# A reordered output phase: row maxima, moments, convolution and merge take other places in their engines' queues

## The reference, cut to what matters

```python
b, n, d = x.shape                       # 16 images, 4096 tokens, 128 channels
h, m, dh = (8, 64, 16)                  # heads, landmarks, width of a head
sim1 = jnp.einsum('bhid,bhjd->bhij', q, k_l)
attn1 = jax.nn.softmax(sim1, axis=-1)
out = attn1 @ attn2_inv @ (attn3 @ v)   # the last two factors: 64 x 16 a head, made earlier
res = conv_general_dilated(v, conv_w, ...)   # 33 taps along the tokens, a filter a head
out = out + res
out = out.transpose(0, 2, 1, 3).reshape(b, n, h * dh)
return x + (out @ w_out + b_out)
```

## Time and profile before

| | us |
|---|---|
| median of 3 runs | 5909.45 |
| the profiled execution, its own time | 5913.64 |
| its span | 5911.8 |
| output phase, first to last reciprocals of full slots | 2542.9 to 3561.8 |
| TensorE busy in the whole span | 5253.6 |
| ScalarE busy in the whole span | 3138.0 |
| VectorE busy in the whole span | 3071.2 |

### The profile page before, as it was taken

The page is one execution under the profiler, slowest core; times in us unless marked ns, Lnnn a source line. Parts: engine busy times, 40 slices in busy tenths (PEclk is TensorE's granted clock), DMA queues, the critical chain, the costliest instruction groups (busy, mean ns, idle before and its releaser), DMA issues. The chain is left out here.

```text
span 5911.8 us, 223297 instructions
## 1 busy us (share of the span) xinstructions
PE 5253.6 (89%) x97395; PEld 3278.2 (55%) x97488; DVE 3071.2 (52%) x8152; ACT 3138.0 (53%) x9108; POOL 1523.0 (26%) x1905
## 2 busy tenths in 40 slices
PE   5599999997899998799999997888888888888888
PEld 4599888896566666744444444333333333333333
DVE  8677777775788886568888883111111111111111
ACT  6465555565677776378888883333333333333333
POOL 2100000002888874256666662000000000000000
PEclk7899999999999999999999998999999999999999
DMA  9631111225777773467777762111111111111100
GB/s 389 270 115 58 58 58 60 84 77 183 245 245 243 231 243 105 102 175 203 202 203 202 204 173 66 33 34 32 32 34 33 32 32 35 32 32 32 35 18 24
DMA packets 773031, 689.32 MB, mean 117 GB/s; under 512 B 67056, under 2 KB 663024, under 8 KB 767984
## 3 DMA queue, kind: packets, MB, share of 16 engines
q1 hardware_dynamic: 754672, 575.39, 32.6%
q0 software_dynamic: 14672, 95.16, 4.0%
q10 hardware_dynamic: 2736, 4.89, 0.2%
HBM read 392.17 MB, written 274.89 MB: 113 GB/s over the span
## 5 line engine op out<-in xcount | busy, mean ns | idle before, releaser
L2797 ACT ACTIVATE f_y<-f_acc 128x16 f32<-128x16 f32 x4096 | 754.7, 184 | 1542.5 <-PE f_acc L2739 1542.5
L2739 PEld LDWEIGHTS f_acc<-f_y,f_vT 128*32 128x32 f32 x32768 | 645.2, 108 | 1438.7 <-ACT f_y L2797 1437.0
L2739 PE MATMUL f_acc<-f_y,f_vT 128*32 128x16 f32 x32768 | 1046.1, 193 | 279.6 <-issue 1.5
L2697 PE MATMUL f_junk<-f_idle 128*32 128x512 bf16 x8400 | 832.5, 376 | 0.0
L2579 DVE COPY f_zT<-f_zt 128x512 f32<-128x512 f32 x124 | 85.8, 692 | 1138.4 <-PE f_zt L2653 1138.4
L2355 DVE TENSOR_REDUCE o_m<-o_bank_l 128x8 bf16<-128x512 f32 x512 | 329.7, 686 | 132.4 <-PE o_bank_l L2152 130.0
L2572 DVE TENSOR_SCALAR f_wxn<-f_wxp,f_scale,f_shift 128x512 f32<-128x512 f32 x126 | 102.1, 811 | 509.0 <-PE f_wxp L2667 508.9
L1299 ACT ACTIVATE a_p<-a_s 128x512 f32<-128x512 f32 x502 | 259.3, 602 | 153.0 <-PE a_s L1166 151.2
L2318 ACT ACTIVATE o_p<-o_bank_s 128x512 f32<-128x512 f32 x512 | 264.4, 602 | 142.0 <-PE o_bank_s L2175 142.0
L533 POOL DMA_DIRECT2D hidden<-l_h x46 | 34.7, 756 | 1162.1 <-DVE l_hsum L790 961.6
L712 ACT ACTIVATE l_gate<-l_pf,r_ctx 128x256 f32<-128x256 f32 (+7 forms) x512 | 202.5, 446 | 229.1 <-PE l_pf L643 228.8
(11 more groups left out here) (323 smaller groups left out, 11517.6 us busy)
## 6 DMA issues: line engine op xcount, KB each, us to landing
o_v<-vals SPq DMA_DIRECT2D x256, 272.0 KB, 3.4
a_hid<-hidden SPq DMA_DIRECT2D x112, 520.0 KB, 5.0
hidden<-l_h POOLq DMA_DIRECT2D x46, 1040.0 KB, 6.6
l_x<-skew SPq DMA_DIRECT2D x46, 1024.0 KB, 5.2
vals<-a_v SPq DMA_DIRECT2D x128, 272.0 KB, 3.4
gn_x<-in_x SPq DMA_DIRECT2D x16, 2048.0 KB, 17.4
a_xin<-in_x SPq DMA_DIRECT2D x128, 256.0 KB, 5.1
tokens<-a_t SPq DMA_DIRECT2D x128, 256.0 KB, 3.4
```

The source lines that it names most:

```text
L2697: nc.tensor.matmul(junk[rows, :], idle[:, 0:QUAD], idle[:, :], start=True, stop=True)
L2739: mm = nc.tensor.matmul(acc[k % 2][rows, t, :], vT[:, rows], before, start=False, stop=True, skip_group_check=True)
L2797: nc.scalar.activation(y[q][:, step, :], acc[step // RC % 2][:, step % RC, :], ACT.Sigmoid).then_inc(s_y, 1)
```

## The change

Four things move; no instruction is added or taken away.

1. TensorE: the first half of `row_maxima` comes before `scores`; `moments` and `convolve` come before `weigh` instead of at the end; `turn_maxima` comes before `queries`. As the convolution now precedes `weigh`, it has a wait of its own for the first three exponentials, since it overwrites `bank_s[2]`.
2. ScalarE: `copy_convolved` comes before `copy_weighed`, `negate` before `copy_queries`.
3. VectorE: `merge` of chunk c-1 comes before `reciprocals` of chunk c-1 instead of at the end of the slot.
4. After the last slot `merge` and `reciprocals` swap in the same way.

```diff
@@ TensorE
             def slot(b, c, q, first, last):
-                scores(b, c, q)
                 nq = q if c + 1 < NG else 1 - q
                 if follows(c, 1, last):
                     row_maxima(b, c + 1, 0, nq)
+                scores(b, c, q)
                 if precedes(c, 3, first):
                     project(b, c - 3)
                 if follows(c, 1, last):
                     row_maxima(b, c + 1, 1, nq)
+                if precedes(c, 4, first):
+                    moments(b, c - 4)
+                if not last:
+                    wait(pe, "exp", PAIRS_H * nth(b, c) - 1)
+                    convolve(b + 1, c, bank_conv[:, :])
                 weigh(b, c, q)
+                if follows(c, 1, last):
+                    turn_maxima(b, c + 1)
                 if follows(c, 3, last):
                     queries(b, c + 3)
-                if follows(c, 1, last):
-                    turn_maxima(b, c + 1)
-                if not last:
-                    convolve(b + 1, c, bank_conv[:, :])
                 if precedes(c, 2, first):
                     turn_convolved(b, c - 2, q if c >= 2 else 1 - q)
-                if precedes(c, 4, first):
-                    moments(b, c - 4)
@@ ScalarE
+                if not last:
+                    copy_convolved(b + 1, c, 1 - q, bank_conv[:, :])
                 copy_weighed(b, c)
+                if follows(c, 1, last):
+                    negate(b, c + 1)
                 if follows(c, 3, last):
                     copy_queries(b, c + 3)
-                if follows(c, 1, last):
-                    negate(b, c + 1)
-                if not last:
-                    copy_convolved(b + 1, c, 1 - q, bank_conv[:, :])
@@ VectorE
                 if precedes(c, 1, first):
+                    merge(b, c - 1)
                     reciprocals(b, c - 1)
                 if precedes(c, 2, first):
                     normalise(b, c - 2)
                     add_convolved(b, c - 2)
-                if precedes(c, 1, first):
-                    merge(b, c - 1)
@@ VectorE, after the last slot
             residual(B - 1, NG - 3)
+            merge(B - 1, NG - 1)
             reciprocals(B - 1, NG - 1)
-            merge(B - 1, NG - 1)
```

## The result

The changed kernel takes 5947.33 us (median of 4 runs, 5929.85 to 5951.33), the kernel before 5909.9 (median of 4). The ratio is 1.0055, interval [1.0042, 1.0068]: slower, as forecast, 5 us under the 5952 given. The profiled execution of the changed kernel was its fastest run: 5929.85 us, span 5928.1.

A forecast was written before the change was run, and what follows sets the result against it. Bound: TensorE's 8.10 us a slot, 0.53 of it waits, and a chain through DRAM closing once a slot. -13 - 4 + 41 + 19 = +43 on 5913.64 gives 5957, less 4.2: 5952 us; 8-in-10 range 5892 to 5985.

The forecast's parts named there:

- The 0.53 us of waits: TensorE's waits for the row maxima's reduction and the last exponential go, 0.53 us a slot: pace 8.10 to 7.57.
- The copies behind weigh: Scores wait for the queries' copy, now fourth on ScalarE behind `weigh`: 0.06 us lost a slot, pace 7.63.
- The turn through DRAM: Reciprocals, spread, pack and next reciprocals close once a slot: plain slots 8.03 us instead of 8.15, 13 us gained over 112.
- The early convolution: In 29 slots 0 and 4 TensorE waits about 2.5 us for v; 1.4 each on the path, 41 us lost.
- The clock: TensorE's granted clock falls behind the waits for v in 12 slots, 1.6 us each: 19 us lost, bounds 0 and 46.
- The sum: Whole kernel: -13 - 4 + 41 + 19 = +43 us, giving 5957 against the profiled execution and 5952 as median.
- the rival without the clock: Convolution stands waiting for v as forecast, but TensorE's clock stays up: 5933 us, about 25% chance.
- The merge: On VectorE, merge ahead of the reciprocals is free where these wait for DMA, adds 0.8 us where VectorE is late.
- v is not late enough: At the convolution, v lands at the median 3.4 us; loss 17 balances gain 17: no change, 5909 us, 18% chance.
- the DRAM turn paces and nothing else: The convolution's wait in slots 0 and 4 never delays the next reciprocals; 17 us gained, 5892 us, 13% chance.

The follow-up runs named there:

- the spread's landing late: Changed kernel with v issued before the spread, 1.0205; v behind the pack and one slot earlier, with the late convolution 1.0209, with the changed order 1.0207.
- the three faster orders: v issued one slot earlier in the changed kernel, 0.9969, in the late convolution, 0.9965, and in the kernel before with only its convolution moved early, 0.9966.
- the filler: Changed kernel plus six overwritten 512-column products on TensorE ahead of the convolution in slots 0 and 4 of each image; 5929.49 us, ratio 1.0045 to the kernel before.
- the second profile: Changed kernel without further edits, timed again on another chip beside the kernel before; median 5939.04 us, ratio 1.0051, phase 1052.8 us.
- the late merge: Changed kernel with the merge of chunk c-1 back behind `add_convolved` at the end of VectorE's slot; 5926.58 us, ratio 1.0040 to the kernel before.
- the late convolution: Changed kernel with the convolution back behind the queries and its ScalarE copy behind `copy_queries`; 5880.91 us, ratio 0.9964 to the kernel before.

## Why the prediction was right, step by step

**The 0.53 us of waits.** Gone, as predicted: the weight loads' waits for the maxima fell from 142 to 2.

**The copies behind weigh.** Predicted a loss of 0.06 us a slot and a plain pace of 7.63; measured 0.26 + 0.17 = 0.43, of which 0.13 come back since turn and queries now take 1.15 us instead of 1.28 (2669.45 to 2670.60), and 7.88. This term was mis-sized, and the greater of the two waits, that of the first row maxima for the negated maxima, is not in the prediction at all; it had only that of the scores for the queries' copy. I had counted 0.05 us from the end of a copy to the product that it releases, as it is behind the exponentials. The negated maxima, started at 2670.60 with 0.60 us, end at 2671.20, and the row maxima start at 2671.46: 0.26. The queries' copy, started at 2671.08 with 0.62 us, ends at 2671.70, and the scores start at 2671.95: 0.25. Why it is 0.25 here and 0.05 behind the exponentials stays open; in both places the wait stands in front of a weight load.

**The turn through DRAM.** This step failed for the changed kernel. Predicted were plain slots of 8.03 us, paced by the turn. Measured were 7.88 in the mean of 87 slots, TensorE's own pace with the copies' waits, and only 19 times in the 96 slots 1 to 3 and 5 to 7 did the reciprocals wait for their denominators. Three such slots and one with a standstill take 3 x 7.88 + 10.03 = 33.7 us, 8.42 each, which leaves room for the turn. It shows once v comes a slot earlier: this kernel's reciprocals are 7.95 us apart in the mean, with 67 waits of 40.9 us, though its engines could do 7.87. So the turn's mean is near 7.9 to 8.0, a little better than I took. That it can pace the phase is shown by lengthening it: with the spread's landing late the kernels are 1.5 to 2.5% slower than the same ones without that edit. No run made it shorter. That the three faster orders end at 0.9965 to 0.9969 because of it is therefore an inference from these waits.

**The early convolution.** The mechanism is the one predicted. I had put the convolution's start S at 6.3 us after the reciprocals that `project` waits for (5.5 to 7.6), and the reciprocals after the next ones 11.18 us behind it. Over the 29 slots S is 6.19 in the mean (5.5 to 7.9). The second distance is 11.05 in the median; it exceeds 12 us six times, five of them where the clock fell. In the slot shown, the convolution starts at 2659.53, and on VectorE:

```profile
2661.41 0.35 DVE L2387 RECIPROCAL o_rec_packed<-o_den_packed 128x32 f32<-128x32 f32 x1 [0.18 <-DMA o_den_packed<-o_odd]
...
2670.58 0.35 DVE L2387 RECIPROCAL o_rec_packed<-o_den_packed 128x32 f32<-128x32 f32 x1
```

2670.58 - 2659.53 = 11.05, and no wait stands in front: VectorE was late, the denominators were not. The slots with a piece of v took 10.03 us, where the sum has 8.03 + 1.4 + 19 / 29 = 10.1. The standstills themselves are shorter, 1.63 us (47.2 / 29) instead of 2.5. I had TensorE run ahead of the turn, wait at `project` and start it 1.70 us after the reciprocals; it is not ahead, and starts it 2.55 us after them in the median. The net amount: the changed kernel against the one with v a slot earlier is 1.0051 - 0.9969 = 0.82% or 48 us for 29 events, 1.7 us each (with what the clock adds), where I had 41 + 19 = 60. The phase of 1055.3 us against 1001.5 says 54.

**The clock.** Predicted 12 falls of 1.6 us, 19 us in all. The one fall read in detail cost 1.5 us. There were five in one profile of the changed kernel and six in the other, so some 8 us: the term was about twice too large. That the waits for v cause them is shown by the counts, one with the filler and none in the same order with v a slot earlier. The slower runs are another matter. They have a mean clock lower by 0.003 to 0.004, which at 1.7 us each would be 10 to 14 more falls, and the predicted term would fit them if these lay in the phase. But the second profile (5936.11 us, mean clock 0.978) has about nine more stretches of 3.4 us at half the clock than the first, and only two of the nine lie in the phase, which is 2.5 us shorter than in the first although the span is 6.3 longer. So what makes some runs slower lies mostly outside the phase, and its cause stays open.

**The sum.** By the prediction's terms the 29 slots lose 56 us against the kernel before, the plain ones gain 10 and the last image 4, together +43 with rounding. The profile has +50, -23 and -3: +24, and the second profile of the changed kernel +22. The medians have +37 and, on the other chip, +32. So the direction, the mechanism and the price of a slot with v came out, but that 5952 is only 5 us from 5947 is partly luck: the gain of the plain slots was put too low, and runs that are slower outside the phase made up for it. The phase alone would give 5934, which is the number of the rival without the clock.

**The merge.** I priced its new place at 0.8 us in each of 29 events, 23 us of the 41. In the slots 0 and 4 the late merge does give back 19.4 us, but the other slots take most of it, and 7 us are left in the time. So the new place costs about what I said, and the old place has a price that I had not seen at all: beside GpSimd the merge takes 0.6 us longer with the late convolution, and there it is on the path of nearly every slot. (VectorE's terms in the prediction add up to 7.4 us, not 7.5; no other number is worked out from that sum.)

**The rivals.** "v is not late enough" and "the DRAM turn paces and nothing else" are out for the changed kernel, but the second is what happens once v comes a slot earlier, 17 us predicted for it, 18 measured. The Trainium skill ("DMA: Bandwidth & Descriptors", Anatomy of one DMA) gives about 2.0 us plus bytes over 436 GB/s as a fit for transfers issued from GpSimd; the prediction used it for SyncE's. By it v would have been in time. The measurement decides against it here: v's median landing is 3.4 us in both kernels.

## What to carry to other kernels

A reordering that removes waits in every slot can still lose by one that it makes in every fourth, if that one sits in front of a loop that closes through DMA: look up, for each instruction that moves forward, when its latest input was issued, not only whether its engine was busy. When it loses so, try the data's issue one slot earlier at the same place in the queue before giving the order up. And keep the large transfers away from the front of a small one whose landing something waits for.

## What the runs showed of the hardware

- The landing of two 8 KB transfers depends on what was issued ahead of them: the broadcast behind them goes 2.4 us after their issue where v stands behind them, and 4.95 us after in a slot with 1.3 MB in front. Moving a 544 KB load by one place in SyncE's queue cost 1.5% of the program (1.0205 against 1.0051).
- The granted clock fell to 0.50 behind a stretch of 3.41 us in which TensorE was busy 1.73, and in the kernel before behind 3.40 us with 1.73; the fall read in detail cost 1.5 us of TensorE's time. Between 2530 and 3540 us it did not fall before the change, fell five and six times after, and once with the waits for v filled.
- One VectorE operation on 128x512 f32 took 0.72 us where it started while GpSimd was idle. At the end of the slot with the late convolution, where 125 of 128 started while GpSimd was busy, it took 1.36 us in the mean, and 0.85 us at the end of the slot in the kernel before.
- From the end of a copy on ScalarE to the product on TensorE that waited for it passed 0.25 and 0.26 us, and 0.05 us from the end of the last exponential to `weigh`.
